# A decoder block on one core: later routing, longer buffer rings and a shorter front

## The reference

```
h = layernorm(x) * (1 + ca) + sa
w = (h @ Wqkv.T) in 16 heads of 16;  Pi = softmax over the heads of normalised w*w
x = x + ga * ( -(w * Pi) / (1 + dots) @ Wout.T + bout )          # the "front"
X = layernorm(x) * (1 + cb) + sb
nx = rmsnorm(X) * g1;  Q = 4 heads of 64;  one K and one V of 64 channels
X = X + softmax(Q K^T / 8) V @ Wo.T                                # the "loop"
nx = rmsnorm(X) * g2;  rw = softmax(nx @ Wr.T + bias);  top 2 of 8 experts
X = X + swiglu_shared(nx) + sum of the 2 experts' swiglu * weight  # the "tail"
out = x + gb * X
```

## Time and profile before

| | us |
|---|---|
| median of three runs | 1437.05 |
| profiled execution | 1436.41 |
| its span | 1434.5 |
| granted clock, mean | 0.957 |
| PE busy | 1270.5 (89%) |
| DVE busy | 1089.7 (76%) |
| ACT busy | 892.1 (62%) |
| POOL busy | 350.4 (24%) |

### The profile page before, as it was taken

One profiled execution on the slowest core, in us unless ns is written; L12 is line 12 of the kernel. 1 busy time (PEld: TensorE's weight loads), 2 busy tenths in 40 slices (PEclk: granted clock), 3 DMA queues, 4 the chain that ended last, 5 costly groups with the idle time before them and its releaser, 6 DMA issues.

```text
span 1434.5 us, 18743 instructions
## 1 busy us (share of the span) xinstructions
PE 1270.5 (89%) x5896; PEld 905.9 (63%) x5896; DVE 1089.7 (76%) x2076; ACT 892.1 (62%) x1450; POOL 350.4 (24%) x381
## 2 busy tenths in 40 slices
PE   4777676899999999999998999999877799999994
PEld 2334544566666666676765666766545687887783
DVE  4957877687988877888878888888833757547688
ACT  2355565577776766776787766676636656555451
POOL 0443340112211121110212211111272001723346
PEclk9889787899999999999999999999979899999998
DMA  5000017100000000000000001000020423655644
GB/s 199 8 1 37 23 59 242 56 8 6 4 9 4 5 9 4 5 9 4 9 4 4 9 4 56 9 5 28 22 84 27 145 63 106 200 155 171 184 128 147
DMA packets 61376, 80.71 MB, mean 56 GB/s; under 512 B 12002, under 2 KB 51682, under 8 KB 61026
## 3 DMA queue, kind: packets, MB, share of 16 engines
q1 hardware_dynamic: 36384, 46.81, 10.1%
q0 software_dynamic: 10752, 21.18, 5.4%
q10 hardware_dynamic: 14146, 11.52, 2.4%
HBM read 41.79 MB, written 37.62 MB: 55 GB/s over the span
## 4 chain that ended last, share of the span: by engine, by line
PE 57%; DVE 10%; POOL 5%; DMA 4%; ACT 3%; issue 3%; SPq 2%; POOLq 0%; ACTq 0%; DVEq 0%
PE PS L1819 8%; PE PS L1748 7%; PE PS L1751 7%; PE PS L1766 6%; PE PS L1768 6%; PE PS L1767 6%; PE PS L1716 6%; PE PS L1845 4%; DVE mx L1161 4%; DVE PL L1190 3%; POOL xbuf L1540 2%; SPq L633 2%; POOL y L1552 2%; PE PS L1803 1%; PE PS L1702 1%
## 5 line engine op out<-in xcount | busy, mean ns | idle before, releaser
L777 ACT ACTIVATE PT<-PS 128x1024 f32<-128x1024 f32 x256 | 262.4, 1025 | 211.0 <-PE PS L1751 210.8
L1161 DVE TENSOR_REDUCE mx<-PS 128x1 f32<-128x512 f32 x512 | 336.9, 683 | 67.2 <-PE PS L1716 66.1
L1190 DVE TENSOR_TENSOR PL<-PT,PH 128x1024 fp32r<-128x1024 f32 x256 | 317.8, 1242 | 13.2 <-ACT PH L780 12.8
L780 ACT ACTIVATE PH<-PT 128x1024 fp32r<-128x1024 f32 x256 | 271.6, 1061 | 8.1
L1766 PE MATMUL PS<-PH,VH 128*65 128x512 f32 x512 | 215.1, 420 | 10.6 <-DVE PL L1190 8.8
L1768 PE MATMUL PS<-PL,VH 128*65 128x512 f32 x512 | 205.0, 400 | 0.0
L1767 PE MATMUL PS<-PH,VL 128*65 128x512 f32 x512 | 204.4, 399 | 0.0
L1716 PE MATMUL PS<-KA,Q 128*128 128x512 f32 x384 | 156.5, 418 | 9.6 <-DVE mx L1161 6.0
L1748 PE MATMUL PS<-Q,KA 128*128 128x512 f32 x384 | 129.2, 418 | 13.0 <-DMA Q<-mT 11.1
L1751 PE MATMUL PS<-Q,KB 65*128 65x512 f32 x384 | 123.0, 402 | 0.0
L1515 POOL DMA_DIRECT2D z_scratch<-OZ x32 | 17.6, 550 | 386.5 <-ACT OZ L789 386.5
(11 more groups left out here) (243 smaller groups left out, 2502.6 us busy)
## 6 DMA issues: line engine op xcount, KB each, us to landing
xbuf<-xT SPq DMA_DIRECT2D x26, 384.0 KB, 4.9
xg<-xbuf SPq DMA_DIRECT2D x78, 128.0 KB, 2.3
ybuf<-yo ACTq DMA_DIRECT2D x78, 128.0 KB
nxT<-in_wexp SPq DMA_DIRECT2D x9, 768.0 KB, 4.4
x<-in_x SPq DMA_DIRECT2D x8, 512.0 KB, 11.9
x_scratch<-x SPq DMA_DIRECT2D x2, 2048.0 KB, 7.3
Z<-z_scratch POOLq DMA_DIRECT2D x32, 128.0 KB, 3.1
nxT<-x_scratch SPq DMA_DIRECT2D x32, 128.0 KB
```

The lines of the kernel that those rows point to most:

```text
L777: act.activation(PT[:, gs % 4, :], PS[:, bk:bk + 2, :].rearrange("p a n -> p (a n)"), ACT.Exp, scale=0.125).then_inc(sem("pt"), 1)
L780: act.activation(PH[:, gs % 4, :], PT[:, gs % 4, :], ACT.Copy).then_inc(sem("pt_h"), 1)
L1161: dve.tensor_reduce(mx[:, qb % 2, i, c:c + 1], PS[:, k, :], AX, ALU.max).then_inc(sem("dve_out"), 1)
L1190: dve.tensor_tensor(PL[:, gs % 4, :], PT[:, gs % 4, :], phf[:, gs % 4, :], ALU.subtract).then_inc(sem("pl"), 1)
```

## The change

1. The scaling `nx_scale` moves from DVE to ACT.
2. Three of the first head pair's four query blocks (`q_mm`, `q_hi`, `q_lo` 0 0 1 to 3) and the first seven maxima of query block 1 leave the front and go to the first steps of the loop; `front_done` waits for less.
3. A step's V products wait for PL only ahead of the third one.
4. The last 512 queries (head 3 of batch 1) are not divided before the projection: `proj_even` adds the other head's part in the loop, and `proj_last` multiplies the undivided O and its sum of weights (65 rows) by a 65x257 matrix, after which DVE takes the reciprocal of column 256 and multiplies and adds. The way over DRAM for that block is gone, eight of the sixteen norms move into the loop, and the root stands in iteration 1 (before: 4).
5. The 24 jobs of the weight splits start in iteration 1 at 1.7 for each (before: 4 at 2.5), and POOL makes the down part's remainder (128x512) instead of DVE.
6. The router's 48 logit jobs start in iteration 13 at 2.4 (before: 5 at 2.5), its choice and row numbers in 34 (before: 25), and the scatter runs in iterations 44 to 51 at 2 for each (before: 34 to 49 at 1).
7. The routed tiles get a ring of 8 of their own (before: 4 shared with the others), fetched nine iterations ahead (before: four), and the results a ring of 7 (before: 3). The stores of the results are issued by SP (before: ACT), ahead of the iteration's fetch.

```diff
+NXR = 8
+NYO = 7
...
-rsqrt2 5; k_mm 0 3; q_hi 0 0 0; q_lo 0 0 0; v_mm 0 3; squares 6; max_mm 0 0 0 0; shift2 7; q_mm 0 0 1;
-max_mm 0 0 0 1; max_mm 0 0 0 2; q_hi 0 0 1; q_lo 0 0 1; rsqrt2 6; max_mm 0 0 0 3; max_mm 0 0 1 0;
...
+rsqrt2 5; k_mm 0 3; q_hi 0 0 0; q_lo 0 0 0; v_mm 0 3; squares 6; max_mm 0 0 0 0; shift2 7;
+max_mm 0 0 0 1; max_mm 0 0 0 2; rsqrt2 6; max_mm 0 0 0 3; max_mm 0 0 1 0;
+max_mm 0 0 1 1; squares 7; max_mm 0 0 1 2; max_mm 0 0 1 3; max_mm 0 0 2 0;
+max_mm 0 0 2 1; rsqrt2 7; max_mm 0 0 2 2; max_mm 0 0 2 3; max_mm 0 0 3 0;
+max_mm 0 0 3 1; max_mm 0 0 3 2; max_mm 0 0 3 3; max_row 0 0; max_turn 0 0;
...
-    return pairs([("choose", b)] * 20, n) + pairs([("count", b)] + [("place", b)] * 24, n)
+    choose = [("choose", b)] * 22
+    return (pairs(choose[:3], 3) + pairs(choose[3:16], n) + pairs(choose[16:19], 3) + pairs(choose[19:], 3)
+            + pairs([("count", b)] + [("place", b)] * 24, n))
...
-        maxima += spread(max_jobs(n // 4, n % 4), 24 * (n - 1) - 8, 24 * (n - 1) + 15)
-    maxima = [x for x in maxima if x[1] not in FRONT]
+        maxima += spread(max_jobs(n // 4, n % 4), 24 * (n - 1) - 8 if n > 1 else 3, 24 * (n - 1) + 15)
...
+    projections = [x for x in projections if x[0] < 8 * 96]
+    projections += spread([("proj_even", i) for i in range(12, NT)], 7 * 96 + 60, 7 * 96 + 90)
...
+        if bh == 0:
+            todo += spread(q_jobs(0, 0)[3:6], 0, 2.5) + spread(q_jobs(0, 0)[6:], 5, 17)
...
+            todo += spread(norm_jobs(1)[:4], 74, 84) + spread(norm_jobs(1)[4:8], 86, 95.5)
...
-    norm = norm_jobs(1)
-    last = [[x for j, p in enumerate(proj_jobs(3, qb)) for x in (norm[4 * qb - 8 + j], p)] for qb in (2, 3)]
-    side = [(-2, 9, [("z_out", 7, 3)] + last[0]),
-            (0, 1, [("z_inv", 7, 3), ("z_back", 7, 3)]),
-            (3, 9, last[1] + norm[8:]),
-            (4, 2.5, [j for ex in range(NE) for j in split_jobs(ex)]),
-            (5, 2.5, rlog_jobs(1)),
-            (25, 1, route_jobs(1, 5) + scatter_jobs(1)),
+    norm = norm_jobs(1)[8:]
+    side = [(-2, 9, proj_jobs(3, 2)),
+            (-1, 9, [x for i in range(4) for x in (("proj_last", 12 + i), norm[i])]),
+            (0, 3, norm[4:]),
+            (1, 1.7, [j for ex in range(NE) for j in split_jobs(ex)]),
+            (13, 2.4, rlog_jobs(1)),
+            (34, 1, route_jobs(1, 5)),
+            (44, 2, scatter_jobs(1)),
             (NT + NTI + 3, 0.5, combine_jobs(0)),
             (NT + 2 * NTI + 1, 1, combine_jobs(1))]
...
+    rest = nxT[:, :, :].rearrange("p c n -> p (c n)")[:, 0:12 * D].rearrange("p (s d) -> p s d", d=D)
+    late = W[0][:, 1, 1, 2 * 768:2 * 768 + 2 * D].rearrange("p (s d) -> p s d", d=D)
+    xr = [late[:, 0, :], late[:, 1, :]] + [rest[:, i, :] for i in range(6)]
+    yr = [yo[:, i, :] for i in range(3)] + [rest[:, 6 + i, :] for i in range(4)]
     wsh = KA0[:, 0:2 * 768].rearrange("p (c n) -> p c n", c=2)
...
+    wol = W[0][0:65, 1, 1, 2 * 768:2 * 768 + 257]
...
-                w.wait_ge(sem("w_lo"), 3 * (k - 1))
+                w.wait_ge(sem("w_up"), 2 * (k - 1))
+                w.wait_ge(sem("w_down"), k - 1)
...
-            q = s % NXG
-            experts_free(w)
-            if s >= NXG:
-                w.wait_ge(sem("tx"), s - NXG + 1)
+            keys_free(w)
+            pe_of(w, ("proj_last", NT - 1, 0))
+            if nth[s] % NXR >= 2:
+                w.wait_ge(sem("w_up"), 2 * (NE + 1))
...
+            x_free(w, s)
             for r in range(NSX):
                 w.wait_ge(sem(f"d_sx{r}"), 32 * scattered(g, r))
             w.wait_ge(sem("d_zero"), 16 * 26)
-            sp.dma_start(xg[:, q, :], xbuf[g][i * P:i * P + P, :]).then_inc(sem(f"d_xg{q}"), 16)
+            sp.dma_start(x_slot(s), xbuf[g][i * P:i * P + P, :]).then_inc(sem(f"d_xr{nth[s] % NXR}"), 16)
+        def store(s):
+            g, i = TILES[s]
+            if g is None:
+                return
+            r = nth[s] % NYO
+            w.wait_ge(sem("yo"), nth[s] + 1)
+            sp.dma_start(ybuf[g][i * P:i * P + P, :], yr[r]).then_inc(sem(f"d_y{r}"), 16)
...
-                fetch(s + 4)
+            if 0 <= s - 2 < NTL:
+                store(s - 2)
+            if s == NT - 6:
+                for t in range(2):
+                    fetch(NT + t)
+            if s == NT - 2:
+                for t in range(6):
+                    fetch(NT + 2 + t)
+            if NT - 2 < s and s + 9 < NTL:
+                fetch(s + 9)
...
+        def nx_scale(b, i):
+            n = b * NT + i
+            w.wait_ge(sem("h2"), n // 4 + 1)
+            nx_free(w, n)
+            act.activation(nx[:, n % NNX, :], X2[:, n, :], ACT.Copy, scale=rs2[:, n:n + 1]).then_inc(sem("nx"), 1)
...
-            k, r = nth[s], nth[s] % 3
+            k, r = nth[s], nth[s] % NYO
             w.wait_ge(sem("down"), s + 1)
-            if k >= 3:
-                w.wait_ge(sem(f"d_y{r}"), 16 * (k // 3))
-            act.activation(yo[:, r, :], PS[:, 5 + s % 2, 0:256], ACT.Copy).then_inc(sem("yo"), 1)
-            w.wait_ge(sem("yo"), k + 1)
-            act.dma_start(ybuf[g][i * P:i * P + P, :], yo[:, r, :]).then_inc(sem(f"d_y{r}"), 16)
+            if k >= NYO:
+                w.wait_ge(sem(f"d_y{r}"), 16 * (k // NYO))
+            if r >= 3:
+                w.wait_ge(sem("w_up"), 2 * (NE + 1))
+                w.wait_ge(sem("w_down"), NE + 1)
+            act.activation(yr[r], PS[:, 5 + s % 2, 0:256], ACT.Copy).then_inc(sem("yo"), 1)
...
+        def proj_last(i):
+            n, k = NT + i, banks.bank["proj_last", i, 0]
+            pe_of(w, ("proj_last", i, 0))
+            pe_of(w, ("max_turn", 7, 3, 0))
+            mark(dve.reciprocal(m16[:, 0, i - 12:i - 11], PS[:, k, 256:257]))
+            w.wait_ge(own, made[0])
+            out_of(w, ("proj_even", i, 0))
+            dve.scalar_tensor_tensor(X2[:, n, :], PS[:, k, 0:256], m16[:, 0, i - 12:i - 11], X2[:, n, :], ALU.mult,
+                                     ALU.add).then_inc(sem("dve_out"), 1)
...
+        def split_down(ex):
+            k = order.index(ex)
+            hi, lo = (wsh, wsl) if ex == NE else (wh[:, ex, :, :], wl[:, ex, :, :])
+            w.wait_ge(sem("w_hi"), 3 * k + 3)
+            after_last("w_down")
+            pool.tensor_tensor(lo[:, :, 512:768], wst[:, k % 2, :, 512:768], hi[:, :, 512:768].bitcast(F32),
+                               ALU.subtract).then_inc(sem("w_down"), 1)
...
+        def proj_last(i):
+            w.wait_ge(sem("d_wol"), 16)
+            w.wait_ge(sem("o"), 32)
+            k = bank("proj_last", i, 0)
+            pe.matmul(PS[:, k, 0:257], OZ[:, (i - 12) * P:(i - 11) * P], wol, start=True,
                       stop=True).then_inc(sem("pe_use"), 1)
...
-            low_done(w, gs)
...
             pe.matmul(PS[0:65, 4, :], VH[:, t, :], PH[:, h, c], start=first, stop=False)
             pe.matmul(PS[0:65, 4, :], VL[:, t, :], PH[:, h, c], start=False, stop=False)
+            low_done(w, gs)
             pe.matmul(PS[0:65, 4, :], VH[:, t, :], PL[:, h, c], start=False, stop=last).then_inc(sem("av"), 1)
...
         def split_x(s):
-            g, q = TILES[s][0], s % NXG
-            if g is None:
+            if TILES[s][0] is None:
                 w.wait_ge(sem("xg"), nth[s] + 1)
             else:
-                w.wait_ge(sem(f"d_xg{q}"), 16 * fetched(s))
+                w.wait_ge(sem(f"d_xr{nth[s] % NXR}"), 16 * (nth[s] // NXR + 1))
             if s:
...
-            w.wait_ge(sem("w_lo"), 3 if TILES[s][0] is None else 3 * (NE + 1))
+            w.wait_ge(sem("w_up"), 2 if TILES[s][0] is None else 2 * (NE + 1))
...
+            w.wait_ge(sem("w_down"), 1 if TILES[s][0] is None else NE + 1)
```

More of the change, by code:

```diff
@@ L165, in loop_order @@
     for n in range(1, 32):
-        maxima += spread(max_jobs(n // 4, n % 4), 24 * (n - 1) - 8, 24 * (n - 1) + 15)
-    maxima = [x for x in maxima if x[1] not in FRONT]
+        maxima += spread(max_jobs(n // 4, n % 4), 24 * (n - 1) - 8 if n > 1 else 3, 24 * (n - 1) + 15)
     projections = []
     for pair in range(4):
-        for qb in range(4 if pair < 3 else 2):
+        for qb in range(4 if pair < 3 else 3):
             at = 192 * pair + 96 + 24 * qb + 48
             projections += spread(proj_jobs(pair, qb), at, at + 78 if pair < 3 else at + 23)
+    projections = [x for x in projections if x[0] < 8 * 96]
+    projections += spread([("proj_even", i) for i in range(12, NT)], 7 * 96 + 60, 7 * 96 + 90)
+    projections.sort(key=lambda x: x[0])
     for bh in range(8):
@@ L519, in stored, with x_slot, x_free @@
     def stored(b, r):
-        return sum(k % 3 == r for k in range(NTI * (b + 1)))
-    def fetched(s):
-        return sum(t <= s and t % NXG == s % NXG for t in routed)
+        return sum(k % NYO == r for k in range(NTI * (b + 1)))
+    def x_slot(s):
+        return xg[:, nth[s] % NXG, :] if TILES[s][0] is None else xr[nth[s] % NXR]
+    def x_free(w, s):
+        ring, n = (shared, NXG) if TILES[s][0] is None else (routed, NXR)
+        if nth[s] >= n:
```

(28 more changed lines are left out.)

52 lines of the change are left out of this document (21 added, 31 removed), and 2 rows, old and new, of the table READERS.

## The result

The changed kernel takes 1445.13 us (median of 4, 1444.39 to 1445.97) against 1436.6 (1434.51 to 1437.35): ratio 1.0052, interval 1.0032 to 1.0072. It is slower by about 8.5 us.

A forecast was written before the change was run, and what follows sets the result against it. PE was taken to bound the loop and the tail, with gaps at the front's end and in the first sixteen tiles. Gains in front, loop and tail against the scatter's +26.7 summed to +0.4, giving 1437.4 us, range 1426 to 1447.

The forecast's parts named there:

- the likeliest case: Whole kernel: the scatter's stall before tile 55 eats what the rest gains, 1437.4 us, chance 0.45.
- rival 2: Early tail: the weight buffers' cycle becomes the bound and ACT and PE wait before tile 14; +7, 1444, chance 0.15.
- rival 3: Loop start: moved front jobs replace the zero fills as what delays mT, chain 5 us longer; +5, 1442, chance 0.10.
- Scatter of batch 1: Tail, tiles 46 to 55: POOL's scatters at 1.27 us each start late and delay tile 55's fetch; +26.7 us.
- Front and its zero fills: Front to step 8: front ends 10 us sooner, zero fills and mT follow; -10, with -1.4 for PE's shorter gap.
- they are DVE's: ... make 19.2, together 238 to 243: Loop start: block 1's maxima, counted as DVE work, are ready at 238 to 243, before the zero fills end at 243.7.
- `nx_scale`: Front: sixteen scalings take 5.5 us off DVE and add as much on ACT; 3 us of gain booked.
- Loop: Attention loop: most of PE's 8.8 us of waits for PL goes, but proj_even and norms come in; -1 us.
- Tiles 0 to 15: Early tail: less waiting for the last norm's root (-7.7, tiles 0 to 7), router logits leave (-6.3, tiles 8 to 15).
- the case in which every one meets: Early tail: all eight POOL down splits hold DVE's up split, 8 to 14 us of DVE; nothing charged for it.
- Logits, choice, tile 18: Tail from tile 16: logits come back +4.0, the router's choice is better spread -1.5, tile 18's fetch waits +1.5.
- Late fetches: Tail after tile 55: PE's three waits for xbuf rows vanish with fetches nine iterations ahead; -5.9 us.

The follow-up runs named there:

- run 1: The changed kernel with only its tail table reset: logits from iteration 8 at 3, router from 24, batch 1's scatter from 35 at 1 each; ratio 0.9905.
- run 2: The kernel before with router from iteration 34 and batch 1's scatter from 44 at 2 for each iteration; ratio 1.0129.
- run 5: The changed kernel with run 1's early scatter table and the 26 zero fills spread seven at a time behind the loop's mT transfers; 1422.58 us, ratio 0.9895.
- run 6: As run 5, with the order of the front, first maxima and queries put back as before the change; 1413.04 us, ratio 0.9828.
- run 12: The kernel of run 6 with the first seven maxima of block 1 moved into the loop, queries left in the front; ratio 0.9865.
- run 3: The changed kernel with the order of the front, first maxima and queries as before, the scaling staying on ACT; ratio 1.0027.
- run 7: The kernel before with only the scaling nx_scale moved from DVE to ACT; 1436.25 us, ratio 0.9991.
- run 11: The kernel of run 6 with the wait for PL back in front of all three V products; ratio 0.9812.
- run 8: The kernel of run 1 (zero fills in one piece) with routed rows fetched five iterations ahead instead of nine; 1423.11 us, ratio 0.9896.

## Why the forecast came out as it did

The forecast was +0.4 us on the profiled execution; it was +9.6. The time lies in the range (1426 to 1447), but the likeliest case was not the one that happened, and the outcome that came, slower, had 0.34 where faster had 0.40. That the time is inside is in part luck: the range reaches 1447 by rival 2 (1444, the nearest number), whose mechanism did not happen. The nearest in mechanism is rival 3, which I had at 1442.

- **Scatter of batch 1**: right in mechanism and size, +26.7 forecast, +26.5 measured. Its parts (4.85, 39.5, 2.65, 2.47) came out as 4.77, 39.84, 2.54, 2.13. Runs 1 and 2 show it by removing it from the one kernel and putting it into the other. The seven result buffers did no harm: tile 52's copy ran at 1275.94, behind the turn of tile 55 at 1271.75.
- **Front and its zero fills**: here the forecast failed. The front ended 8.7 us sooner, near the 10; but step 10 was only 3.6 us ahead, 7.8 short of the 11.4. Of the 7.8, 1.3 are the front's end and 6.5 the chain behind it. The failing step is "they are DVE's: ... make 19.2, together 238 to 243". I added up DVE's rows and gave the wait for others a few microseconds. The moved query blocks are a chain over engines (product on PE, for the most part at the lower clock, copy on ACT and POOL, remainder on DVE, and only then the maximum's product on PE), and three of them stand in the loop's first steps between score products that ACT needs. It took 35.3 us from the front's end, not 19.2 + 4. Rival 3 had the mechanism and said 5, for a chain longer by 5; the chain was longer by 12, and step 10 came 6.5 later. Runs 5, 6 and 12 show it.
- **`nx_scale`**: booked as 3 of the 10; no gain is shown (0.1 and 0.6 us at the front's end in runs 3 and 7), and up to 3 us are not excluded (run 7). Three of the sixteen in the front were stretched on DVE, to 2.43, 1.52 and 2.06 us. The moved jobs make most of the front's gain: beside the same scaling on ACT the moved front ends at 214.8 in the mean of four executions, and the old order at 223.2 in the mean of six.
- **Loop**: -1 forecast, -0.5 measured, and neither stands out of the noise: the same stretch takes 812.1 to 818.2 us in the other kernels, and run 11 shows no price for the wait for PL, so of the 8.8 us of the earlier trace rows none is shown to be won.
- **Tiles 0 to 15**: -14.0 forecast, -14.7 measured, divided otherwise (-6.3 and -8.4). Weight waits in tiles 8 to 15 were 0.2 to 1.0 us each, so rival 2 did not happen. The logits' part is seen again in runs 5, 6 and 8, where they start in iteration 8: tiles 0 to 15 take 58.0 to 58.6 us and tiles 16 to 45 86.8 to 86.9, where the change has 50.8 and 91.2. No run takes the new last projection (part 4) or the earlier splits (part 5) alone, so their shares are not divided. The rule of the Trainium skill ("SBUF — State Buffer", "SBUF: two separate sides") is that a DVE operation with two SBUF inputs and a GpSimd operation that reads SBUF exclude each other. The trace of the changed kernel agrees: DVE's up split is 0.75 us alone and 1.27 in the row that begins at 1101.10, while POOL's split runs from 1100.54 for 1.28:

```profile
1101.10 1.27 DVE L1414 SCALAR_TENSOR_TENSOR wl<-nxT,g2c,wh 128x512 fp32r<-128x512 f32 x1 [0.65 <-ACT wh L884]
1103.63 0.74 DVE L1414 SCALAR_TENSOR_TENSOR wl<-nxT,g2c,wh 128x512 fp32r<-128x512 f32 x1
```

  Three of eight splits held DVE's in this way, 0.2 to 0.5 us each, and not the 8 to 14 us of the case in which every one meets. In three others DVE's had begun first, and it was POOL's split that took longer, 1.69 to 1.85 us instead of 1.28.
- **Logits, choice, tile 18**: +4.0 together forecast, +4.7 measured.
- **Late fetches**: -5.9 + 2 for the clock, measured -3.9. The waits of the earlier trace rows are gone; why is open between the ring and the stores (run 8 excludes only the distance of nine).
- **The end**: +1.0, not explained.

## What to carry to other kernels

When a stage has a producer with a fixed rate (here a queue that took 1.27 us for each indirect DMA on one chip, and up to 1.73 on two others, with their stops), starting it later by n tiles costs n tiles unless the consumer's slack is as large, and issuing its work more densely changes nothing: compute the producer's last item from the rate, not from the table. Work moved out of a serial stretch is worth its time only if it doesn't become a chain in the place where it lands; count the engines that a moved job visits, with their waits, and not the busy time of one. A transfer that stands behind unrelated ones in a queue is found by what released the first wait after it: spreading 26 zero fills was worth more than all of the front's moves.
